# A fused attention and mixture-of-experts kernel: maxima columns by their own DMAs, row-tiled projections, earlier switch to attention

## The chip, the cores and the metric

The kernel runs on one core of one Trainium2 chip. The metric is the device time of one execution in microseconds (us). A core has a matrix engine (PE, with its weight loads PEld), a vector engine (DVE), a scalar engine (ACT), GpSimd (POOL), and SyncE (SP), which here does nothing but issue DMAs; a queue name with a q (SPq, POOLq) is the issuing side of that engine. Sixteen DMA engines carry all transfers.

## What is computed

```python
def reference(x, ...):                  # x: 8 x 1024 x 256
    xn = layernorm(x)
    s  = attn(xn)                       # layernorm with scale and bias, low-rank q and kv (128),
                                        # 16 heads of 64, rotary turn of q and k,
                                        # softmax(q k^T / 8) v, times w_out, plus the residual
    g  = silu(ffn(xn))                  # 8 experts, top 2 of them, capacity 1.25, 256 -> 1024 -> 256
    return x + s * g
```

All inputs and the output are float32.

## The kernel before, in words

The program has four stages on one core. A projection stage (`project_parts`, `pj`) normalises the tokens and writes the low-rank products, the values and the router's logits. Attention (`attend_parts`, `at`) follows from about 235 to 2650 us. The experts (`expert_parts`) and the combination follow. The routing arithmetic (`route_parts`, `rt`) is spread through the start of attention: it is a generator, and each `next(choice)` in the tensor and vector streams runs one piece.

Attention works on 64 pairs of heads (`NPAIR`, 8 batches by 8 pairs). The two heads of a pair lie on the upper and lower 64 partitions, so their matrix products run beside each other as row tiles of the array. A pair has 1024 queries in two halves (`bank`, n = 0 and 1) and 8 key tiles (`KT`), which gives 16 units u. For each unit PE computes the scores of both heads into `st[u % 2]` (`scores`, L1329), each score as three products of high and low parts (`hi`, `lo`). ACT takes the exponential into `ex` (`exps`, L1171), DVE adds the exponentials up over the keys (`add_keys`, L1035), and PE multiplies them by the values into `pv[n]` (`values`, L1366). POOL's accumulating DMAs join the two partial sums, PE turns them into denominators (L1425), SP spreads these over the partitions and back (`spread`, `broadcast`, L855 and L862), and DVE divides (`normalise`).

The loop over pairs is software-pipelined. `body(i, prev, ahead)` has eight steps, g = 0 to 7, called slots in the change's name. Each holds units 2g and 2g+1, the values of two earlier units, and two half-steps (`step_x`, `step_y`, L1387 and L1401) of another chain: for each of 8 tiles of 128 queries it finds a bound on the scores of each query, to be subtracted before the exponential. That chain goes differ (PE, `fr`), relu (`gain`, ACT L1197), add (PE), and a row maximum (`maximum`, DVE L1028, line L1033), which writes one column of `mx`, 128 partitions by 1. In body i the slots 6 and 7 of pair i run at g = 0 and 1, and slots 0 to 5 of pair i+1 at g = 2 to 7 (`slot_of`). Each slot has a column for each head: 16 columns a pair. In what follows, the two maxima of a slot are the one for head 0, at the slot's own g, and the one for head 1, one g later.

From columns to rows: when four slots (eight columns, one bank) are there, `turn_maxima` multiplies `mx[n]` by an identity on PE, into the free corner of a `pv` bank; `negate` on ACT copies it with its sign changed into `mneg`; and `max_rows` on SP (L848) sends it by two DMAs of four rows of 512 bytes into one partition for each head of `top`. The first score unit of a bank waits for that (`s_mrow`, in `scores_free`), and the first two units of each half have a fourth product, `one_row` times `top`, that adds the bound.

Projections: `body(i)` makes the keys of pair i+2 and the queries of pair i+3 out of the low-rank products. Each has two halves. The first half is a full 128-row product of three passes (`project`, PE at g = 1 for keys, at g = 5 for queries). The second half is done as row tiles beside scores (`split`, `upper_rows`, `lower_rows`, at g = 3 and g = 7): the upper and the lower 64 rows of the projection go out one after the other, each beside a score product on the other half of the array. `proj_copy` on ACT takes a half out of its `pv` bank, which must be free.

SP issues its DMAs in program order: in `body`, the loads of queries for pair i+3 (weights `w`, low-rank products `c`), the values `v` of pair i+1, the four rows of bank 1, the loads of keys for i+3, `spread` of the pair before, the rows of bank 0 of pair i+1, and at the end the store and the `broadcast` of the pair before. Within `broadcast` SP waits until the reciprocals have landed in memory, then reads them back.

Of the kernel before, what the change touches and what calls it, by code (L numbers as in the profile page):

```python
# [595 lines left out]
def route_parts(nc, ctx, keep, pj):  # L596

    with ExitStack() as tiles:
# [106 lines left out]

        def ranked(e):
            e.wait_ge(s_done, 1)
# [7 lines left out]
        return {"vector": vector, "scalar": scalar, "tensor": tensor, "ranked": ranked, "spread": spread, "done": done}  # L715


def attend_parts(nc, ctx, below, bridge, io, scr, keep, pj, rt):


    with ExitStack() as tiles:
# [27 lines left out]
        mneg = [sb(f"mneg{n}", [2 * QB, P], F32R) for n in range(NH2)]  # L749
# [3 lines left out]
        ones, osb, den, denc, recc, rec, oT, ident_r = (bridge[n] for n in ("ones", "osb", "den", "denc", "recc", "rec", "oT", "ident_r"))  # L753
# [19 lines left out]
        s_tf, s_neg = sem("tf"), sem("neg")  # L773
# [9 lines left out]
        route_at = [st[0][:, n, :] for n in range(2)]  # L783
# [48 lines left out]
        def sync(e, pj_value, pj_compressed, ex_sync):  # L832
# [15 lines left out]
            def max_rows(j, n):  # L848
                e.wait_ge(s_neg, j.n(2, n + 1))
                for h in range(2):  # L850
                    r = rows[h].start
                    e.dma_start(top[j.u][r:r + 1, bank[n]].bitcast(F32).rearrange("o (t q) -> o t q", q=P),
                                mneg[n][h * QB:(h + 1) * QB, :].bitcast(F32)).then_inc(s_mrow[n], 16)
# [21 lines left out]
            def prologue():  # L875
                for s in s_store:
                    e.sem_inc(s, 16)
                for t in range(TB):
                    pj_value(t)
                    if t == 1:  # L880
                        pj_compressed()
                pj["stored"](e)
                pj["values_stored"](e)
                load_v(At(0, 0))
                for x in (Q, K):
                    e.wait_ge(s_pr, projected(At(0, 0), x, 1))
                    load_w(At(0, 2), x)
                    e.sem_inc(s_ld[x][0], 16)
                e.wait_ge(s_init, 2)
                max_rows(At(0, 0), 0)  # L890
# [95 lines left out]
        def vector(e, ex_vector):  # L986
# [41 lines left out]
            def maximum(j, k, h, ready):  # L1028

                if k % QB == 0 and h == 0:  # L1030
                    wait(e, s_tf, j.n(2, k // QB - 1))
# [36 lines left out]
            def prologue():  # L1068
# [8 lines left out]
                for h in range(2):  # L1077
                    r = rows[h].start
                    last = e.memset(one_row[r:r + 1, :].bitcast(F32), 1.0)
                last.then_inc(s_init, 1)  # L1080
                e.tensor_copy(ident_r[:, :], keep["ident"][:, :]).then_inc(s_init, 1)
# [20 lines left out]
                for _ in range(3):  # L1102
                    next(choice)

            def body(i, prev, ahead):
# [3 lines left out]
                for g in range(NG):  # L1109
# [25 lines left out]
                    if g == 5 and most:  # L1135
                        turn_sin(two, K)
# [33 lines left out]
        def scalar(e, pj_value, ex_scalar):  # L1170
# [41 lines left out]
            def negate(j, n):  # L1212
                e.wait_ge(s_tf, j.n(2, n + 1))
                wait(e, s_mrow[n], j.n(32, 0))
                e.activation(mneg[n][:, :], pv[n][0:2 * QB, 0:P], ACT.Copy, scale=-1.0).then_inc(s_neg, 1)

            def prologue():
# [22 lines left out]
                for k in range(6):  # L1240
# [3 lines left out]
                    if k == 4:  # L1244
                        negate(first, 0)
                    if k == 5:
                        proj_copy(third, Q, 0, pv[1])
# [5 lines left out]
                proj_copy(third, Q, 1, pv[1])  # L1253
                pj["values_stored"](e)

            def body(i, prev, ahead):
                one, two, three = (i.next(d) for d in (1, 2, 3))
                more = ahead >= 1
                for g in range(NG):
                    if g == 1 and prev:  # L1260
                        out_copy(prev, 1)
# [26 lines left out]
                    if g == 1 and more:  # L1288
                        far_keys(one)
                    if g == 2 and more:  # L1290
                        high(one, K)
# [18 lines left out]
        def tensor(e, pj_value, ex_tensor):  # L1310
# [11 lines left out]
            def scores_free(i, u):  # L1322
                if u == 0:
                    e.wait_ge(s_lo, i.n(2, 2))
                if u % KT == 0:
                    e.wait_ge(s_mrow[u // KT], i.n(32, 32))
# [9 lines left out]
            def project_row(j, x, k, h, dst):  # L1336
                ws, cs = PASSES[k]
                return e.matmul(dst[:, :], w[x][j.u][rows[h], ws, :], c[x][rows[h], cs, bank[1]],
                                start=(h + k == 0), stop=(ws == 1), skip_group_check=(h == 1))

            def upper_rows(i, u, j, x, dst):

                scores_free(i, u)
                for k in range(3):
                    mm = project_row(j, x, k, 0, dst)
# [10 lines left out]
            def lower_rows(i, u, j, x, dst):  # L1356

                e.wait_ge(s_upper, i.n(2, 1 if x == K else 2))
                for k in range(3):
# [3 lines left out]
                    mm = project_row(j, x, k, 1, dst)  # L1363
# [47 lines left out]

            def turn_maxima(j, n):
# [956 lines left out]
```

## Time and profile before

| | us |
|---|---|
| median of 3 runs | 3684.16 |
| lowest and highest of the three | 3682.55, 3687.47 |
| the profiled execution | 3679.85 |
| span of its trace | 3678.3 |

| engine | busy, us | share of the span |
|---|---|---|
| PE | 3609.8 | 98% |
| PEld | 2361.3 | 64% |
| DVE | 3195.8 | 87% |
| ACT | 2763.5 | 75% |
| POOL | 1201.5 | 33% |

Busy times of an engine are of instructions that execute; waits for semaphores aren't in them. On DVE and ACT an instruction's shown duration overlaps its successor's by some tens of ns, so the sum of durations is more than the busy time. PE durations (0.39 us for a product of 512 columns) overlap far more; what a product costs is the distance from one start to the next. All times in windows and timelines count from the start of the span.

### The profile page before, as it was taken

The page shows a single profiled execution, that of the slowest core. Times are in us where ns is not written, and L with a number is a line of the kernel's source. Part 1 is how long each engine was busy: PE and PEld are TensorE (multiplying, and loading weights), DVE is VectorE, ACT ScalarE, POOL GpSimd, SP SyncE. Part 2 cuts the span into 40 slices and gives each one's busy share as a digit, 9 for nine tenths or more (in the row PEclk, how much of TensorE's full clock was granted, in tenths as well). Part 3 has the DMA queues.
Part 4 walks back from the last instruction along what each step waited for, and adds up shares of the span by engine and source line. Part 5 has one row for each costly group of instructions (what it writes and reads, how often), then busy time and mean ns, then how long its engine had stood idle before and what let it go on. Part 6 is the DMA issues. An engine that isn't in the chain of part 4 may idle for free. (4 is left out here: it accounts for less than half of the span.)

```text
span 3678.3 us, 77202 instructions
## 1 busy us (share of the span) xinstructions
PE 3609.8 (98%) x24217; PEld 2361.3 (64%) x24217; DVE 3195.8 (87%) x4341; ACT 2763.5 (75%) x4016; POOL 1201.5 (33%) x1178
## 2 busy tenths in 40 slices
PE   7989999999999999999999999999999999999999
PEld 5754444444444444444444444444699999999999
DVE  8869999999999999999999999999777777777799
ACT  5767888888888888888888888888666666666665
POOL 2202222222222222222222222222366666666500
PEclk9999999999999999999999999999999999999999
DMA  7975666666666666676766666665566666665798
GB/s 266 356 261 136 176 168 172 171 170 169 167 172 164 179 161 182 156 184 156 186 158 182 162 174 164 174 170 142 177 219 216 225 213 213 225 215 214 240 370 275
DMA packets 378436, 724.74 MB, mean 197 GB/s; under 512 B 105277, under 2 KB 253886, under 8 KB 342272
## 3 DMA queue, kind: packets, MB, share of 16 engines
q0 software_dynamic: 83504, 340.66, 36.0%
q1 hardware_dynamic: 294864, 383.23, 31.5%
q8 instruction: 35, 0.57, 0.1%
q14 instruction: 33, 0.27, 0.0%
HBM read 453.60 MB, written 138.81 MB: 161 GB/s over the span
## 5 line engine op out<-in xcount | busy, mean ns | idle before, releaser
L1176 ACT ACTIVATE at_ex<-at_st 128x1024 f32<-128x1024 f32 x1024 | 1047.7, 1024 | 195.7 <-PE at_st L1319 185.6
L1375 PE MATMUL at_pv<-at_ex,at_v 128*64 128x512 f32 x4096 | 991.6, 605 | 0.0
L1033 DVE TENSOR_REDUCE at_mx<-at_fr 128x1 fp32r<-128x512 f32 x1024 | 705.2, 689 | 227.6 <-PE at_fr L1385 179.2
L1200 ACT ACTIVATE at_fr<-at_fr 128x512 f32<-128x512 f32 x1024 | 601.2, 587 | 208.6 <-PE at_fr L1385 191.1
L1375 PEld LDWEIGHTS at_pv<-at_ex,at_v 128*64 128x64 f32 x4096 | 248.3, 136 | 470.5 <-issue 461.5
L1046 DVE TENSOR_TENSOR at_sum<-at_sum,at_ex 128x1024 f32<-128x1024 f32 x448 | 544.9, 1216 | 3.7 <-ACT at_ex L1176 3.4
L1319 PE MATMUL at_st<-at_qh,at_kh 64*128 64x512 f32 x2048 | 460.1, 399 | 9.9 <-DMA at_top<-at_mneg 2.7
L1385 PE MATMUL at_fr<-at_kfar,at_qh 64*128 64x512 f32 x1024 | 454.6, 444 | 5.9 <-DVE at_mx L1033 5.3
L1382 PE MATMUL at_fr<-at_kdif,at_qh 64*128 64x512 f32 x1024 | 456.3, 446 | 3.5 <-DVEq L674 2.5
L1382 PEld LDWEIGHTS at_fr<-at_kdif,at_qh 64*128 64x128 f32 x1024 | 188.3, 184 | 416.3 <-issue 359.5
L1319 PE MATMUL at_st<-at_ql,at_kh 64*128 64x512 f32 x2048 | 452.6, 391 | 0.0
L1319 PE MATMUL at_st<-at_qh,at_kl 64*128 64x512 f32 x2048 | 451.7, 390 | 0.0
L1913 PE MATMUL ex_o<-ex_w,ex_hT 128*128 128x256 f32 x3408 | 426.0, 285 | 0.9 <-DVE ex_out L1778 0.9
L1897 PE MATMUL ex_h<-ex_xT,ex_w 128*128 128x256 f32 x3408 | 421.1, 283 | 1.6 <-DVE ex_w L1731 1.6
L1897 PEld LDWEIGHTS ex_h<-ex_xT,ex_w 128*128 128x128 f32 x3408 | 414.1, 192 | 2.8 <-DVE ex_w L1731 1.4
L1913 PEld LDWEIGHTS ex_o<-ex_w,ex_hT 128*128 128x128 f32 x3408 | 413.2, 192 | 1.1 <-DVE ex_out L1778 1.1
L934 POOL DMA_DIRECT2D at_rotq<-at_swpq x126 | 111.4, 1030 | 858.2 <-DVE at_swpq L1001 857.6
L1831 ACT ACTIVATE ex_w<-seam_stage 128x1024 fp32r<-128x1024 f32 x142 | 142.9, 1053 | 285.9 <-PE ex_o L1913 281.7
L1703 POOL DMA_INDIRECT scr_eo<-ex_out,mid_slots x142 | 255.1, 1796 | 213.8 <-DVE ex_out L1778 178.8
L1046 DVE TENSOR_TENSOR at_sum<-at_ex 128x1024 f32<-128x1024 f32 x224 | 272.4, 1216 | 4.4 <-ACT at_ex L1176 4.4
L1319 PEld LDWEIGHTS at_st<-at_qh,at_kh 64*128 64x128 f32 x2048 | 216.7, 185 | 66.6 <-issue 35.0
L928 POOL DMA_DIRECT2D at_sum<-at_sum x95 | 88.6, 933 | 496.8 <-DVE at_sum L1046 473.5
(213 smaller groups left out, 6345.0 us busy)
## 6 DMA issues: line engine op xcount, KB each, us to landing
at_cq<-scr_c SPq DMA_DIRECT2D x62, 1024.0 KB, 6.2
at_ck<-scr_c SPq DMA_DIRECT2D x62, 1024.0 KB, 5.0
at_sum<-at_sum POOLq DMA_DIRECT2D x95, 512.0 KB, 6.1
scr_v<-pj_v SPq DMA_DIRECT2D x64, 512.0 KB, 6.9
at_v<-scr_v SPq DMA_DIRECT2D x64, 512.0 KB, 6.7
mid_rec<-scr_rec SPq DMA_DIRECT2D x256, 128.0 KB
scr_o<-mid_oT SPq DMA_DIRECT2D x64, 512.0 KB
at_rotq<-at_swpq POOLq DMA_DIRECT2D x126, 256.0 KB, 4.6
```

What stands on the lines that cost most here:

```text
L1033: e.reduce_max(mx[k // QB][:, h * QB + k % QB:h * QB + k % QB + 1], fr[h][:, :], AX.X).then_inc(s_tr[h], 1)
L1046: e.tensor_tensor(out=acc, in0=ex[k - 1][:, :, :] if first else acc, in1=ex[k][:, :, :], op=ALU.add).then_inc(s_sum, 1)
L1176: e.activation(ex[k][:, :, :], st[u % 2][:, :, :], ACT.Exp, scale=SCALE).then_inc(s_exp, 1)
L1200: e.activation(fr[h][:, :], fr[h][:, :], ACT.Relu).then_inc(s_pos[h], 1)
L1319: return e.matmul(st[u % 2][:, h, :], kk[rows[h], keys], qq[rows[h], bank[n]], start=(t == 0 and kt < 2), stop=(t == score_terms(u)[-1]), ...
L1375: mm = e.matmul(pv[n][rows[h], :], v[i.u][:, kt, rows[h]], ex[kt][:, h, :], start=(kt == 0), stop=(kt == KT - 1))
L1382: return e.matmul(fr[h][:, :], query_tile(j, k, h), kdif[j.u][rows[h], :], start=True, stop=True)
L1385: return e.matmul(fr[h][:, :], query_tile(j, k, h), kfar[j.u][rows[h], :], start=False, stop=True, skip_group_check=True)
L1703: e.indirect_dma_start(out=scr["eo"], out_offset=bass.IndirectOffsetOnAxis(ap=slots[:, g * GT + c:g * GT + c + 1], axis=0), in_=out[g % 2] ...
L1831: e.activation(w2_half(a.u, 0, k), half2(raw2[a.u], k), ACT.Copy).then_inc(s_w2h, 1)
L1897: mm = e.matmul(phid[:, j, f % 2 * GP:(f % 2 + 1) * GP], w1[q][:, ws, f, k, :], xT[q][:, xs, k, :], start=(ws + xs + k == 0), stop=(ws == ...
L1913: mm = e.matmul(po[:, c, 0:D], hT[q][:, hh, f, c * P:(c + 1) * P], w2[q][:, ws, f, :], start=(hh + ws + f == 0), stop=(hh == 1 and f == NF ...
```

## The change

Four things, in the tensor, vector, scalar and SP streams.

1. `turn_maxima`, `negate`, `max_rows`, the tile `mneg` and the identity for it are gone. Instead SP sends each column of `mx` by a DMA of its own as soon as its maximum is made: `max_row`, 128 partitions by one float into 512 contiguous bytes of a row of `top`, 16 for each pair instead of 4. The sign moves into `one_row`, which now holds -1. The scores' wait counts 8 DMAs for each bank, and a maximum that overwrites `mx` waits for its bank's columns.
2. All four half projections of a body are row tiles, at g = 2 and 3 (keys) and g = 6 and 7 (queries). The full products at g = 1 and g = 5 are gone from the body.
3. ACT and DVE work is moved between the steps: the copy of the previous pair's output and the high part of the keys go behind the first relu of their step, the latter to g = 3; the far keys are made one body earlier, at g = 7; `low` of the queries goes from g = 1 to g = 2; at g = 5 the second turn of the keys goes ahead of an addition.
4. Before the first body, SP loads the weights of the third pair's projections after the second value tile, no longer after all stores; PE waits for one piece of the routing (`counted`), not for the rank, and the rank's wait moves to the first values of the first body; one of the routing's PSUM tiles moves from `st` to `pv`.

```diff
@@ sync @@
+            def max_row(j, k, h):
+
+                wait_apart(e, s_tr[h], j.n(NSLOT_Q, k + 1), s_apart_s)
+                r, col = rows[h].start, h * QB + k % QB
+                e.dma_start(top[j.u][r:r + 1, k * P:(k + 1) * P].bitcast(F32), mx[k // QB][:, col:col + 1].bitcast(F32),
+                            allow_slow_non_contiguous=True).then_inc(s_mrow[k // QB], 16)
...
                     if t == 1:
                         pj_compressed()
+                        e.wait_ge(s_made, 4)
+                        for x in (Q, K):
+                            e.wait_ge(s_pr, projected(At(0, 0), x, 1))
+                            load_w(At(0, 2), x)
+                            e.sem_inc(s_ld[x][0], 16)
+                for k in range(6):
+                    for h in range(2 if k < 5 else 1):
+                        max_row(At(0, 0), k, h)
                 pj["stored"](e)
                 pj["values_stored"](e)
                 load_v(At(0, 0))
...
+                one = i.next(1)
                 if ahead >= 3:
                     load(i.next(3), Q)
+                max_row(i, 5, 1)
+                max_row(i, 6, 0)
                 if ahead:
-                    load_v(i.next(1))
-                max_rows(i, 1)
+                    load_v(one)
+                max_row(i, 6, 1)
+                max_row(i, 7, 0)
+                max_row(i, 7, 1)
+                if ahead:
+                    max_row(one, 0, 0)
+                    max_row(one, 0, 1)
                 if ahead >= 3:
                     load(i.next(3), K)
+                if ahead:
+                    max_row(one, 1, 0)
+                    max_row(one, 1, 1)
+                    max_row(one, 2, 0)
                 if prev:
                     spread(prev, (0, 1))
                 if ahead:
-                    max_rows(i.next(1), 0)
+                    max_row(one, 2, 1)
+                    for k in (3, 4):
+                        for h in range(2):
+                            max_row(one, k, h)
+                    max_row(one, 5, 0)
@@ vector body @@
                     if g < 2 or more:
                         maximum(*slot_of(i, g), 0, s_y)
+                    if g == 5 and most:
+                        turn_sin(two, K)
                     for added in late:
                         add_keys(*added)
-                    if g == 1 and more:
+                    if g == 2 and more:
                         low(one, Q)
...
-                    if g == 5 and most:
-                        turn_sin(two, K)
@@ scalar body @@
                     if g < 2 or more:
                         gain(*slot_of(i, g), 0, s_x)
+                    if g == 1 and prev:
+                        out_copy(prev, 1)
+                    if g == 3 and more:
+                        high(one, K)
                     exps(i, 2 * g)
                     if g < 2 or more:
                         gain(*slot_of(i, g), 1, s_y)
+                    if g == 2 and ahead >= 2:
+                        proj_copy(two, K, 0, pv[1])
+                    if g == 6 and ahead >= 3:
+                        proj_copy(three, Q, 0, pv[0])
+                    if g == 7 and ahead >= 2:
+                        far_keys(two)
                     exps(i, 2 * g + 1)
...
-                    if g in (1, 3) and ahead >= 2:
-                        proj_copy(two, K, g // 2, pv[1])
-                    if g == 2:
-                        negate(i, 1)
-                    if g in (5, 7) and ahead >= 3:
-                        proj_copy(three, Q, (g - 5) // 2, pv[0])
-                    if g == 6 and more:
-                        negate(one, 0)
+                    if g == 3 and ahead >= 2:
+                        proj_copy(two, K, 1, pv[1])
+                    if g == 7 and ahead >= 3:
+                        proj_copy(three, Q, 1, pv[0])
@@ tensor @@
                 def split(g):
 
-                    if g == 3 and ahead >= 2:
-                        e.wait_ge(s_neg, i.n(2, 2))
-                        return two, K, pv[1]
-                    if g == 7 and ahead >= 3:
-                        e.wait_ge(s_neg, one.n(2, 1))
-                        return three, Q, pv[0]
...
+                    if g == 2 and ahead >= 2:
                         if prev:
                             e.wait_ge(s_osb, i.n(2, 0))
                         else:
                             e.wait_ge(s_raw[Q], 6)
+                        return two, K, 0, pv[1]
+                    if g == 3 and ahead >= 2:
+                        e.wait_ge(s_raw[K], two.n(2, 1))
+                        return two, K, 1, pv[1]
+                    if g == 6 and ahead >= 3:
+                        e.wait_ge(s_osb, i.n(2, 1))
+                        return three, Q, 0, pv[0]
+                    if g == 7 and ahead >= 3:
+                        e.wait_ge(s_raw[Q], three.n(2, 1))
+                        return three, Q, 1, pv[0]
...
-                    if g == 1 and ahead >= 2:
-                        project(two, K, 0, pv[1])
-                    if g == 2:
...
-                        turn_maxima(i, 1)
...
                 e.wait_ge(s_init, 2)
-                rt["ranked"](e)
+                rt["counted"](e)
```

## Rows read from the trace of the kernel before

**Rows 1.** Windows: stretch, us, busy PE, PEld, DVE, ACT, POOL, PE clock, DMA share, GB/s

```profile
1200.00:1500.00 300.00, 299.01 (x1844) 148.46 (x1842) 273.39 (x325) 245.14 (x357) 74.53 (x88) 1.00 0.66 170
```

**Rows 2.** Timeline of PE (start, us, what): the first product of each step g, one `step_y`

```profile
1207.69 0.49 PE L1382 MATMUL at_fr<-at_kdif,at_qh 64*128 64x512 f32 x1
...
1212.50 0.49 PE L1382 MATMUL at_fr<-at_kdif,at_qh 64*128 64x512 f32 x1
...
1216.58 0.49 PE L1382 MATMUL at_fr<-at_kdif,at_qh 64*128 64x512 f32 x1
...
1218.30 0.39 PE L1385 MATMUL at_fr<-at_kfar,at_qh 64*128 64x512 f32 x1
...
1221.17 0.50 PE L1382 MATMUL at_fr<-at_kdif,at_qh 64*128 64x512 f32 x1
...
1225.57 0.49 PE L1382 MATMUL at_fr<-at_kdif,at_qh 64*128 64x512 f32 x1
...
1230.78 0.50 PE L1382 MATMUL at_fr<-at_kdif,at_qh 64*128 64x512 f32 x1
...
1234.84 0.50 PE L1382 MATMUL at_fr<-at_kdif,at_qh 64*128 64x512 f32 x1
...
1239.43 0.50 PE L1382 MATMUL at_fr<-at_kdif,at_qh 64*128 64x512 f32 x1
```

**Rows 3.** Timeline of PE: what else stands in the steps g = 5, 6 and 1

```profile
1209.74 0.97 PE L1421 MATMUL at_pv<-at_cq,at_wq 128*128 128x512 f32 x3
...
1214.55 0.23 PE L1415 MATMUL at_pv<-mid_ident_r,at_mx 128*8 128x128 f32 x1
1214.71 1.94 PE L1375 MATMUL at_pv<-at_ex,at_v 128*64 128x512 f32 x8
...
1226.37 0.40 PE L1319 MATMUL at_st<-at_qh,at_kl 64*128 64x512 f32 x2
1226.89 0.50 PE L1319 MATMUL at_st<-at_qh,at_kh 64*128 64x512 f32 x2
```

**Rows 4.** Timeline of DVE at g = 5 and the start of g = 6

```profile
1208.23 0.69 DVE L1033 TENSOR_REDUCE at_mx<-at_fr 128x1 fp32r<-128x512 f32 x1 [0.87 <-PE at_fr L1385]
...
1211.70 1.22 DVE L1001 TENSOR_TENSOR at_swpk<-at_rawk,at_sin 128x1024 f32<-128x1024 f32 x1
1213.04 0.69 DVE L1033 TENSOR_REDUCE at_mx<-at_fr 128x1 fp32r<-128x512 f32 x1
```

**Rows 5.** Timeline of SP's queue, same pair: issues of DMAs

```profile
1206.96 3.82 SPq L860 DMA_DIRECT2D mid_denc<-mid_den  x4
...
1225.93 3.27 SPq L869 DMA_DIRECT2D mid_rec<-scr_rec  x4
...
1231.74 0.61 SPq L846 DMA_DIRECT2D at_v<-scr_v  x1
...
1234.71 1.34 SPq L852 DMA_DIRECT2D at_top<-at_mneg  x2
```

**Rows 6.** By tile: issues (min/median/max ns) of two small DMAs

```profile
L852 SPq DMA_DIRECT2D at_top<-at_mneg x256: 572/636/773, 238.1 to 2603.7; - x128
...
L860 SPq DMA_DIRECT2D mid_denc<-mid_den x256: 544/597/2057, 315.6 to 2643.0; - x128
```

**Rows 7.** Windows of 1 us: columns as in Rows 1

```profile
1237.00:1238.00 1.00, 1.00 (x8) 0.38 (x6) 1.00 (x3) 1.00 (x2) 0.00 (x0) 1.00 0.13 40
1283.00:1284.00 1.00, 1.00 (x11) 0.56 (x7) 1.00 (x2) 0.97 (x2) 0.88 (x1) 1.00 0.13 4
```

**Rows 8.** Tile `top`: engines that waited for it over the whole run (us, times)

```profile
  PE at_st L1319: 2.7, 2
```

**Rows 9.** Timelines of PE and of SP's queue where attention begins

```profile
241.23 1.62 PE L1421 MATMUL at_pv<-at_cq,at_wq 128*128 128x512 f32 x3 [6.96 <-DMA at_wq<-scr_w]
...
249.42 0.76 PE L1382 MATMUL at_fr<-at_kdif,at_qh 64*128 64x512 f32 x1 [2.52 <-DVEq L674]
...
236.72 0.70 SPq L834 DMA_DIRECT2D at_wq<-scr_w  x1
```

More of the change, by code:

```diff
@@ L713, in done @@
             e.wait_ge(s_done, 3)
-        return {"vector": vector, "scalar": scalar, "tensor": tensor, "ranked": ranked, "spread": spread, "done": done}
+        return {"vector": vector, "scalar": scalar, "tensor": tensor, "counted": counted, "ranked": ranked, "spread": spread, "done": done}
 def attend_parts(nc, ctx, below, bridge, io, scr, keep, pj, rt):
@@ L782, in attend_parts @@
         Q, K = 0, 1
-        route_at = [st[0][:, n, :] for n in range(2)]
+        route_at = [st[0][:, 0, :], pv[0][:, :]]
         def projected(j, x, n):
@@ L1030, in maximum @@
                 if k % QB == 0 and h == 0:
[L1031 removed]
+                    wait(e, s_mrow[k // QB], j.n(32 * QB))
                 e.wait_ge(ready, j.n(NSLOT_Q, k + 2 - (h == 0)))
@@ L1101, in prologue @@
                         next(choice)
-                for _ in range(3):
+                for _ in range(2):
                     next(choice)
@@ L1244, in prologue @@
                     if k == 4:
-                        negate(first, 0)
+                        proj_copy(third, Q, 0, pv[1])
                     if k == 5:
-                        proj_copy(third, Q, 0, pv[1])
+                        proj_copy(third, Q, 1, pv[1])
                     gain(first, k, 1, s_y)
@@ L1277, in body @@
                         den_copy(prev, 1)
-                    if g in (1, 3) and ahead >= 2:
-                        proj_copy(two, K, g // 2, pv[1])
-                    if g == 2:
-                        negate(i, 1)
-                    if g in (5, 7) and ahead >= 3:
-                        proj_copy(three, Q, (g - 5) // 2, pv[0])
-                    if g == 6 and more:
-                        negate(one, 0)
+                    if g == 3 and ahead >= 2:
+                        proj_copy(two, K, 1, pv[1])
+                    if g == 7 and ahead >= 3:
+                        proj_copy(three, Q, 1, pv[0])
                     if g == 0 and more:
                         high(one, Q)
-                    if g == 1 and more:
+                    if g == 1 and more and not prev:
                         far_keys(one)
-                    if g == 2 and more:
-                        high(one, K)
                     if g == 3 and not more:
@@ L1410, in step_y @@
                 differ(j, k, 1).then_inc(s_y, 1)
-            def turn_maxima(j, n):
-                for h in range(2):
-                    e.wait_ge(s_tr[h], j.n(NSLOT_Q, QB * (n + 1)))
-                e.matmul(pv[n][0:2 * QB, 0:P], mx[n][:, :], ident_r[:, :], start=True, stop=True).then_inc(s_tf, 1)
             def project(j, x, n, dst):
@@ L1472, in prologue @@
                         pj_value(2 * k + 2)
-                    if k in (3, 4):
+                    if k == 3:
+                        e.wait_ge(s_raw[K], 4)
+                        project(third, Q, 0, pv[1])
+                    if k == 4:
                         next(choice)
-                    if k == 4:
+                    if k == 5:
                         e.wait_ge(s_raw[K], 3)
-                        e.wait_ge(s_init, 3)
-                        turn_maxima(first, 0)
+                        next(choice)
                     step_y(first, k)
@@ L1497, in bank_free @@
                         e.wait_ge(s_raw[Q], two.n(2, 2))
+                    elif n == 0 and prev:
+                        e.wait_ge(s_osb, i.n(2, -1))
                     elif n == 0:
-                        e.wait_ge(s_neg, i.n(2, 1))
+                        rt["ranked"](e)
                     elif prev:
@@ L1550, in side @@
                         half_denominators(i, 0)
-                    if g == 6 and ahead:
-                        if ahead >= 3:
-                            e.wait_ge(s_raw[Q], three.n(2, 1))
-                        else:
-                            e.wait_ge(s_osb, i.n(2, 1))
-                        turn_maxima(one, 0)
                 def lagging(u):
```

73 lines of the change are left out of this document (21 added, 52 removed).

## The prediction

> **What bounds the kernel now.** I read the windows first. In 300 us from the middle of attention PE is busy for 299.0, DVE for 273.4 (91%) and ACT for 245.1 (82%), at the full PE clock [rows 1]. PE is the bound, DVE is close behind, and a shorter PE stream can gain little more than a tenth before DVE sets the pace. A busy share doesn't say that PE's time is needed, so the timeline of PE came next, with the first product of each step of `body` [rows 2]. From 1207.69 on the steps are g = 5, 6, 7, 0, 1, 2, 3, and they last 4.81, 4.08, 4.59, 4.40, 5.21, 4.06 and 4.59 us. The reader is to see that they differ, and by what stands in them: g = 5 a full projection, g = 6 and 2 a turn of maxima, g = 7 and 3 a row-tiled projection, g = 1 a full projection and a hole. Third, SP's queue and the sizes of its issues [rows 5, 6], since the change moves the maxima there. Last, the start of attention [rows 9].
>
> **Removed from PE: the turns.** The turn begins at 1214.55 and the values behind it at 1214.71 [rows 3], so it costs 0.16 us. A plain step is then 4.08 - 0.16 = 3.92 (g = 6) or 4.06 - 0.16 = 3.90 (g = 2). 128 turns by 0.16 are 20.5 us, all on PE's path. ACT also loses two small copies a pair; ACT isn't the bound, so that counts nothing.
>
> **Full projections become row tiles.** The full one costs 4.81 - 3.92 = 0.89 (its three products show as 0.97 together, overlapping the next work [rows 3]). The row-tiled one costs 4.59 - 3.92 = 0.67 at g = 7 and 4.59 - 3.90 = 0.69 at g = 3; I take 0.68. The gain is 0.21 for each of 62 key and 61 query halves: 25.8 us.
>
> **The hole at g = 1.** Unit 3's scores start 0.52 us after the product before them (1226.37 to 1226.89 [rows 3]); they stand behind the wait for the output copy that frees `pv[1]`. What g = 1 has beyond a plain step and a full projection is 5.21 - 3.90 - 0.89 = 0.42. The change asks for the same bank one step later, 3.9 us on, when the copy, even one relu (some 0.6 us) later, is long done. 61 bodies by 0.42 are 25.6 us. Sum on PE: 71.9 us, or 1.16 a pair.
>
> **What is late next: DVE at g = 5 and 6.** In g = 5 DVE has a maximum, a turn by the cosine, a maximum, an addition and a turn by the sine. The first starts 0.54 us after the step (1208.23 against 1207.69), and the last ends its slot at 1212.83 (1211.70 plus 1.22 less 0.09 of overlap), 5.14 after the step's start. Today that is in time: the next maximum starts at 1213.04, when PE has made its input [rows 2, 4]. With g = 5 cut to 3.92 that input is there at 3.92 + 0.54 = 4.46, and DVE is 0.68 late. It ends that maximum near 5.75. PE needs it in `step_y` of g = 6, which now is a row-tiled step, and there `step_y` stands 1.72 after the step's start (1216.58 to 1218.30 [rows 2]), so at 3.92 + 1.72 = 5.64. With the hand-over PE waits some 0.25 us. Bounds: 0, if the hand-over is hidden, and 0.68, if PE takes the whole lateness. I take 0.25, nearest to the start times, and 61 by 0.25 are 15.3 us lost. By the same count g = 2 and 3 are just full: DVE has 4.6 us of work in each against 4.6 of PE. ACT's copies and high parts come in steps with at most 4.3 us of work (two relus, two exponentials and 1.45 of the rest) against 4.59; I cost these moves at nothing. Their cover is the distance of one unit between an exponential and the scores that reuse its `st`.
>
> **Added on SP: 16 columns for 4 rows.** No row shows a DMA from 128 partitions to one. The nearest is `mid_denc`, one partition to 128, with 128 short pieces too: 0.60 us in the median of issue, 2.06 at most; the four together took 3.82 here, 0.96 each, the last of them behind full DMA queues [rows 5, 6]. The removed rows took 0.64. A column is then 0.60 to 0.96, and I take 0.60 in quiet stretches. For each pair that is 9.6 to 15.4 us of SP in place of 2.6. What matters is the tightest deadline, bank 1 before the scores at g = 4. Counted from g = 0 (1221.17): the broadcast's last issue ends at 1229.20 (+8.0), and the values' load at 1232.35 (+11.2) [rows 5]. With five columns between and behind, the last is issued by +14.2 at 0.60 each, or +16.0 at 0.96. Its maximum is there by about +10, so SP, not DVE, is last. The scores at g = 4 start at +18.26 now (1239.43) and at +17.5 with the shorter steps (4.40 + 3.90 + 4.58 + 4.59). Before, the last row was issued by 1236.05 (+14.9), and PE waited for rows only twice in the run [rows 8], so issue to landing took under 3.4 us. By 1237 (+15.8) the big loads ahead were through, at a DMA share of 0.13 [rows 7]. At 0.60 a column there are 3.3 us for landing: enough. At 0.96 there are 1.5, and some half a microsecond is missing. I take 0, with 0.5 as the other end. Bank 0 has its last maximum some 8 us before its deadline, ahead of `broadcast` in the queue. Behind SP's new waits stand the key loads, `spread` and `broadcast`; each wait ends before the event that these wait for themselves, and the loads are used a body later.
>
> The DMA engines: the window at 1283 holds only spread pieces of 16 bytes, 4 KB or 256 of them at a share of 0.13 of 16 engines [rows 7], so 0.13 x 16 / 256 = 8.1 ns each. 2048 pieces a pair are 1.04 us of all engines, 3% beside a share of 0.66 [rows 1]. That hides, unless a 4-byte write costs several times a 16-byte one, and no row excludes it.
>
> The Trainium skill, DMA: Bandwidth & Descriptors, Rules for kernel authors, speaks against this part: join many small transfers into one large, and avoid a strided last dimension, which becomes one descriptor for each element. By it the change pays; that is the third rival, and the trace so far bears it out only under full queues.
>
> **The switch.** PE stands 6.96 us for weights that SP issues at 236.72, behind the last stores, and 2.52 more for the rank [rows 9]. After the idle time three products take 1.62 us against 0.97 [rows 3, 9], at the lower of PE's two clock levels. The loads now go out earlier and the rank isn't awaited, so the first body could start near 239, not at 249.4; the limit is then eight columns on SP behind the value stores. But routing pieces move into the first body, where DVE has the most to do. I take 8 us; bounds 3 (most of it given back there) and 13 (the slow clock goes too).
>
> **The sum.** 71.9 - 15.3 + 8 = 64.6 us off the profiled execution's 3679.85 gives 3615.3. The median of the runs lies 4.3 above that execution, so I forecast a median of 3620.
>
> **The rivals.**
> 1. DVE's lateness isn't absorbed: PE pays 0.68 each pair, 41.5 us, and the saving is 71.9 - 41.5 + 8 = 38.4: 3646. For: DVE at 91%, full steps at g = 2 and 3. Against: g = 6 leaves DVE over a microsecond to catch up, and PE needs a maximum only later in the step.
> 2. Columns slightly late: at 0.96 each PE waits 0.5 at g = 4 of each pair, 30.5 us on top of the forecast: 3650. For: the stretch from +8 to +16 has full DMA queues. Against: the median issue of 0.60.
> 3. Columns dear, slower than before: a column costs 1.3 us on SP in that stretch. The last is issued at +11.2 + 6.5 = +17.7, lands 2 us later (an estimate under the 3.4 above) at +19.7, and PE waits 2.2 each pair, 134 us: 3684 - 80 + 134 = 3738. It decides from 1.12 us a column, where the wait, 1.3 us, eats 71.9 + 8. For: the 2.06 of one issue. Against: three of four issues at 0.6.
> 4. Everything hidden, the switch at 13: 84.9 off, 3599.
> 5. The change doesn't take effect, because the hole and DVE's waits move to other steps and use up the gain: 3684. The only thing for it is how close DVE is; its idle 9% speaks against.
>
> **Chances.** Forecast 0.55, rivals 1 to 5: 0.17, 0.10, 0.09, 0.06, 0.03. The forecast's own range is 3605 to 3635 (0 to 0.5 of DVE, 3 to 13 of the switch); with rivals 1, 2 and 4 it is 3598 to 3655. The measurement of this kernel tells 0.2%, 7 us, from no change: faster 0.87, within it 0.04, slower 0.09.
>
> **What would show it.** In the changed trace g = 1 and 5 should last 3.9 us, g = 2, 3, 6 and 7 about 4.6 (g = 6 up to 4.9, with a wait for a maximum), a body 36.2, and the first body should start near 240. A column's issue should be 0.6 us with few waits of PE on `top`. Wrong would be: waits for `top` at g = 4 in each body, issues over 1 us, DVE above 95% with PE waiting at the starts of steps, or ACT ending its exponentials later than the scores that need `st`.

## The result, and the profile after

The changed kernel takes 3785.9 us in the median of four runs (3770.7 to 3803.9) against 3683.4 for the kernel before (3681.4 to 3687.5). The ratio is 1.028, with a 95% interval of 1.023 to 1.033: slower by 102 us, where 64 us less were forecast. Its profiled execution took 3788.99 us with a span of 3787.4. A single run of it scatters by 0.9%, of the kernel before by 0.2%.

The engine rows of the page and the windows of the middle of attention, the latter with the columns of [rows 1]:

```profile
PE 3614.7 (95%) x24458; PEld 2385.7 (63%) x24458; DVE 3181.3 (84%) x4340; ACT 2744.4 (72%) x3888; POOL 1196.4 (32%) x1178
...
1200.00:1500.00 300.00, 283.79 (x1762) 143.16 (x1763) 253.62 (x304) 227.30 (x319) 71.89 (x86) 0.98 0.66 154
```

PE has lost 15 of 299 us to waiting, and its mean clock is 0.98. DVE and ACT are less busy than before, so neither took over as the bound. What PE waits for is in its group of scores (busy, mean ns, then idle before it and the releaser), and in the waits of the whole run (us, times, longest):

```profile
L1333 PE MATMUL at_st<-at_qh,at_kh 64*128 64x512 f32 x2048 | 513.9, 403 | 111.4 <-DMA at_top<-at_mx 111.4
...
PE at_st L1333 <- DMA at_top<-at_mx: 111.4, 61, 9.2
PE at_fr L1401 <- DVE at_mx L1052: 16.3, 68, 2.4
```

The columns are late, once in nearly every body: 111.4 us, where [rows 8] had 2.7. The second line is DVE's lateness, some 0.17 us a body. The timeline of PE around g = 3, 4, 5 and 6 of one body shows where:

```profile
1232.83 0.50 PE L1398 MATMUL at_fr<-at_kdif,at_qh 64*128 64x512 f32 x1
...
1234.77 0.50 PE L1333 MATMUL at_st<-at_qh,at_kh 64*128 64x512 f32 x2 [1.43 <-DMA at_top<-at_mx]
...
1239.89 0.49 PE L1398 MATMUL at_fr<-at_kdif,at_qh 64*128 64x512 f32 x1
...
1243.80 0.50 PE L1398 MATMUL at_fr<-at_kdif,at_qh 64*128 64x512 f32 x1
...
1245.86 0.47 PE L1401 MATMUL at_fr<-at_kfar,at_qh 64*128 64x512 f32 x1 [0.18 <-DVE at_mx L1052]
...
1248.86 0.50 PE L1398 MATMUL at_fr<-at_kdif,at_qh 64*128 64x512 f32 x1
```

The step from 1232.83 to 1239.89 is g = 4, 7.06 us long. PE finished what it had and then stood idle for 1.43 us in front of its scores. The next, g = 5, lasts 3.91, and g = 6 lasts 5.06.

The same reading for some 40 bodies (timelines from 600 to 2100 us, mean distance from one step's first product to the next) gives this table. The last column is of an experiment below.

| step | before | forecast | changed | columns first, addition moved |
|---|---|---|---|---|
| g = 0 | 4.40 | 4.40 | 4.38 | 4.36 |
| g = 1 | 5.21 | 3.90 | 3.91 | 3.93 |
| g = 2 | 4.06 | 4.58 | 4.61 | 4.60 |
| g = 3 | 4.59 | 4.59 | 4.62 | 4.63 |
| g = 4 | 5.40 | 5.40 | 8.19 | 5.37 |
| g = 5 | 4.81 | 3.92 | 3.91 | 3.91 |
| g = 6 | 4.07 | 4.85 | 5.06 | 4.63 |
| g = 7 | 4.60 | 4.60 | 4.60 | 4.60 |
| body | 37.14 | 36.24 | 39.30 | 36.03 |

All steps but g = 4 and 6 came out within 0.04 us of the forecast. The loss is in g = 4: 2.79 us. 1.78 of these are the recorded wait (67.8 us in 38 bodies). Most of the rest is PE's clock. Windows of 2 us around another wait, which ended at 1195.05, show the granted clock (third number from the end) after it:

```profile
1192.00:1194.00 2.00, 1.12 (x6) 0.19 (x2) 2.00 (x4) 1.51 (x3) 0.19 (x1) 1.00 0.91 132
1194.00:1196.00 2.00, 0.95 (x8) 0.84 (x10) 0.98 (x1) 0.00 (x0) 1.59 (x2) 1.00 0.93 370
1196.00:1198.00 2.00, 2.00 (x18) 1.15 (x18) 0.00 (x0) 1.02 (x1) 0.00 (x0) 0.64 1.11 269
1198.00:1200.00 2.00, 2.00 (x12) 0.34 (x12) 1.94 (x3) 1.51 (x2) 0.00 (x0) 0.51 0.68 129
1200.00:1202.00 2.00, 2.00 (x10) 0.61 (x11) 0.48 (x1) 0.67 (x2) 0.89 (x1) 1.00 0.14 21
```

PE waited 1.93 us, and soon after the clock went from 2.4 to 1.2 GHz for over 3 us, in which each product takes twice as long. It doesn't happen each time. The same view behind a wait of 1.94 us, after the row of PE that ends it:

```profile
1474.80 0.50 PE L1333 MATMUL at_st<-at_qh,at_kh 64*128 64x512 f32 x2 [1.94 <-DMA at_top<-at_mx]
...
1474.00:1476.00 2.00, 1.20 (x10) 1.05 (x12) 0.73 (x1) 0.00 (x0) 1.32 (x2) 1.00 0.88 348
1476.00:1478.00 2.00, 2.00 (x18) 0.74 (x16) 0.82 (x2) 1.85 (x3) 0.00 (x0) 1.00 1.06 252
1478.00:1480.00 2.00, 2.00 (x14) 0.56 (x10) 1.60 (x2) 1.18 (x2) 0.42 (x1) 1.00 0.77 138
```

The step of the first of these waits lasts 9.12 us, that of the second 7.57. Of the 38 bodies 18 have the slow stretch, all with waits of 1.82 us or more. The 15 with shorter waits have none, and neither have five with waits of 1.93 to 2.54. In an experiment below it also followed a wait of 1.61, so these runs give no limit. So a wait near 2 us costs 2.2 us of step without the slow clock and 3.7 with it, and on average the slow clock is some 0.8 of the 2.79. The 0.2 left are in each step that waits, with or without the slow clock: 7.06 less 5.40 is 1.66 for a recorded wait of 1.43.

SP's queue in the body of the first timeline (start, us of issue):

```profile
1227.73 0.65 SPq L847 DMA_DIRECT2D at_v<-scr_v  x1
...
1229.88 0.53 SPq L853 DMA_DIRECT2D at_top<-at_mx  x1
```

The second row is the last column of bank 1. It was issued by 1230.41, or +15.1 after g = 0 (1215.29), and landed at 1234.77, or +19.5, when PE went on. The issue is cheap: 0.48 us in the median of 1024. 63 of them took over 1 us, up to 4.5, nearly all the first column behind `spread`, far from the deadline of its bank. The landing is late. In the 38 bodies of the table it came at +19.8 on average, 4.8 us after the issue, and the values' load, which stands ahead in the queue, landed at +19.1.

### The profile page after: what moved, and what is told of

Its sections match the earlier page's. It is cut to its first block and busy times, and to the rows that moved or that the text cites. A ratio compares the mean times of both kernels' runs of the same rounds, so it can differ in the third digit from the quotient of the medians.

```text
span 3787.4 us, 79729 instructions
## 1 busy us (share of the span) xinstructions
PE 3614.7 (95%) x24458; PEld 2385.7 (63%) x24458; DVE 3181.3 (84%) x4340; ACT 2744.4 (72%) x3888; POOL 1196.4 (32%) x1178
## 3 DMA queue, kind: packets, MB, share of 16 engines
q1 hardware_dynamic: 440272, 383.30, 33.9%
## 5 line engine op out<-in xcount | busy, mean ns | idle before, releaser
L1333 PE MATMUL at_st<-at_qh,at_kh 64*128 64x512 f32 x2048 | 513.9, 403 | 111.4 <-DMA at_top<-at_mx 111.4
L1333 PE MATMUL at_st<-at_qh,at_kl 64*128 64x512 f32 x2048 | 509.2, 399 | 0.0
L1333 PE MATMUL at_st<-at_ql,at_kh 64*128 64x512 f32 x2048 | 507.2, 397 | 0.0
L1401 PE MATMUL at_fr<-at_kfar,at_qh 64*128 64x512 f32 x1024 | 464.4, 453 | 17.2 <-DVE at_mx L1052 16.3
L1398 PE MATMUL at_fr<-at_kdif,at_qh 64*128 64x512 f32 x1024 | 465.9, 455 | 1.8 <-DVE at_mx L1052 0.9
L953 POOL DMA_DIRECT2D at_rotq<-at_swpq x126 | 111.4, 1031 | 801.7 <-DVE at_swpq L1020 801.0
L1333 PEld LDWEIGHTS at_st<-at_qh,at_kh 64*128 64x128 f32 x2048 | 241.3, 187 | 164.1 <-issue 117.5
```

Of the source, the lines that this page charges most:

```text
L1333: return e.matmul(st[u % 2][:, h, :], kk[rows[h], keys], qq[rows[h], bank[n]], start=(t == 0 and kt < 2), stop=(t == score_terms(u)[-1]), ...
L1398: return e.matmul(fr[h][:, :], query_tile(j, k, h), kdif[j.u][rows[h], :], start=True, stop=True)
L1401: return e.matmul(fr[h][:, :], query_tile(j, k, h), kfar[j.u][rows[h], :], start=False, stop=True, skip_group_check=True)
```

## The experiments

**The order alone.** All that stands ahead of bank 1's columns on SP goes behind them:

```diff
-                if ahead >= 3:
-                    load(i.next(3), Q)
                 max_row(i, 5, 1)
                 max_row(i, 6, 0)
-                if ahead:
-                    load_v(one)
                 max_row(i, 6, 1)
                 max_row(i, 7, 0)
                 max_row(i, 7, 1)
+                if ahead >= 3:
+                    load(i.next(3), Q)
+                if ahead:
+                    load_v(one)
```

> The changed kernel, with only the order of SP's DMAs in a body changed: the five columns of bank 1 go out ahead of the query loads and of the value load. In the changed kernel step g = 4 lasts 8.2 us on average against 5.4 before, with 1.8 us of PE waiting for columns. Theory 1 (a column can't land before the 1.5 MB of loads queued ahead of it on the same queue; values issued at +12.4 land 6.8 us later, at +19.2, and the scores want the columns at +17.5): the wait is gone, g = 4 lasts 5.4, a body 36.5 us and the whole about 3786 - 61 x 2.8 = 3615 us. Theory 2 (128 pieces of 4 bytes take some 4.3 us to land, whatever stands ahead): the last column, issued near +11.9, lands by +16.2, so the wait is gone here too. Theory 3 (the mass of pieces slows all transfers, wherever they stand): PE keeps waiting over 1 us for columns or for the moved loads, 3700 or more.

Measured: 3633.6 us (3633.0 to 3634.7), ratio to before 0.987 (0.985 to 0.989). g = 4 lasts 5.36 and a body 36.47. Its waits for the columns in the whole run:

```profile
PE at_st L1333 <- DMA at_top<-at_mx: 7.5, 2, 5.8
```

So the wait is a matter of place in the queue, and its end makes the change a gain of 1.3%. The two waits left are those of the first and the last body. Theory 3 falls as it was put, since PE no longer waits. The 19 us above the expectation come from its count: it took 61 times the 2.8 us of the middle bodies, 171 us, but over all 62 bodies between the first and the last the step g = 4 fell by 152 us in sum (484.5 to 332.6), and 3786 less 152 is 3634.

**Only the values behind.**

```diff
                 if ahead >= 3:
                     load(i.next(3), Q)
                 max_row(i, 5, 1)
                 max_row(i, 6, 0)
-                if ahead:
-                    load_v(one)
                 max_row(i, 6, 1)
                 max_row(i, 7, 0)
                 max_row(i, 7, 1)
+                if ahead:
+                    load_v(one)
```

> As the one before, but only the value load (0.5 MB) goes behind the five columns; the query loads (1 MB) stay ahead. Theory 1: the load ahead lands some 6.6 us after its issue at +10, so at +16.6, ahead of the deadline at +17.5: PE waits under 0.3 us in a body, 3615 to 3640. Theory 2: the last column is issued near +14.5 and lands at +18.8, PE waits 1.3 us and more for the clock, near 3700.

Measured: 3659.8 us in one run. g = 4 lasts 5.80 on average, and 16 of some 40 bodies wait, by 0.77 us. Between the two expectations, nearer to the first: both loads count, and the larger share is that of the values, the last one ahead.

**One piece for a column.** The row `one_row` is read in place of the column (the maxima are left out, and the exponential's scale is a thousandth):

```diff
-                e.dma_start(top[...], mx[k // QB][:, col:col + 1].bitcast(F32), ...)
+                e.dma_start(top[...], one_row[r:r + 1, :].bitcast(F32))
```

> The changed kernel with its order of DMAs, but each column DMA reads a constant row of 128 contiguous floats in place of a column (so the real maxima are left out, and the exponential's scale is cut to keep its values finite). The count of DMAs, their bytes and their places in the queue stay, and the 128 pieces of the source are gone. Theory 1: PE waits for these rows as for the columns, 1.8 us in a body, about 3786 us. Theory 2 and theory 3: the waits are gone, about 3615.

Measured: 3653.9 us in one run, g = 4 at 5.60 with 6 waits in 40 bodies. The packets of SP's queue fall from 440272 to 325584, by 112 for each DMA, so it went as 16 pieces, not 128. Theory 1 as it stood, the loads ahead and nothing else, falls: with the same loads ahead most of the waits went. Two causes act together. The values' load ahead also lands sooner here, 5.2 us after its issue in the median against 6.8 in the changed kernel, so the pieces delay that load as well as themselves. By which way they do isn't shown.

**Columns in the kernel before.** Part 1 of the change alone: `max_row` in the change's order, -1 in `one_row`, no turns and no copies of them (waits that counted these copies now count what frees the same bank); the projections stay where they were.

> The kernel before with one part of the change alone: columns sent by their own DMAs in the change's order, no turns, no negated copies; the full projections stay at g = 1 and g = 5. The scores at g = 4 then want their columns at +18.2, not at +17.5. Theory 1: the values ahead of the columns land at +19.2, PE waits about 1 us in a body and pays for the clock after it, less 0.16 us saved twice: 3700 to 3730 us. If the columns cost nothing by themselves and only the shorter steps brought the deadline forward: 3684 - 20 = 3664.

Measured: 3734.0 us (3726.9 to 3743.5), ratio 1.015 (1.013 to 1.017), just above the 3700 to 3730 of theory 1. g = 4 lasts 6.37 against 5.40, with 31 waits in 40 bodies. The steps without their turn last 3.92 (g = 2) and 3.90 (g = 6), which confirms the 0.16 us of a turn. The columns are late without the shortened g = 1. The earlier deadline of the full change then adds to it.

**Landings, measured by SP itself.** A wait behind the last issue of bank 1 makes SP's own waiting the time to landing:

```diff
                 max_row(i, 7, 1)
+                wait_apart(e, s_mrow[1], i.n(32 * QB, 32 * QB), s_apart_s)
```

In the changed kernel, in the one with one piece for a column, in the one with the loads behind, and, after `max_rows(i, 1)` and with a count of 32, in the kernel before:

> The changed kernel with a wait on SP behind the last column of bank 1, so that SP's next issue shows when that column landed. With the loads reordered the waits of PE had gone, and with the 128 pieces of each column replaced by one row most of them had gone too, in the old order. Theory 1 (the loads queued ahead set the landing): from the last issue's end to SP's next issue some 4.4 us, the same as PE saw in the changed kernel (1230.4 to 1234.7). The added wait only moves the key loads, which aren't urgent, so the time stays within 3750 to 3800 us. Rival (what delays the columns is what stands behind them, the key loads that share the DMA engines): with these held back the columns land in 2.5 us and PE's waits shrink, under 3700 us.

> The same wait on SP in the kernel that sends a constant row of 128 contiguous floats in place of each column (real maxima left out, the exponential's scale cut). If the loads ahead set the landing alone, the rows land as late as the columns, 4.4 us after the last issue. If the pieces count, the rows land earlier by their share: PE's waits had fallen from 1.8 us in a body to some 0.2, so 2.5 to 3 us.

> The same wait on SP in the kernel that sends the five columns of bank 1 ahead of the query and value loads. No large load of SP's queue stands ahead now. If the pieces are slow by themselves: over 4 us from the last issue to SP's next. If it is the place in the queue: 2 to 2.5 us. The loads start later by as much; PE should still not wait, 3630 to 3640 us.

> The kernel before with a wait on SP behind the four rows of bank 1, which shows when they land. The prediction allowed under 3.4 us from issue to landing and took the loads ahead to be through at +15.8. In the other runs a column behind the loads landed 3.9 us after its issue (with the key loads held back) and 1.6 us with no load of SP's queue ahead. Theory (rows behind loads are as late as one-piece columns there): 2.5 to 3.3 us from the last row's issue at +14.9, so they land at +17.4 to +18.2, and the kernel before had under 1 us to spare before its scores at +18.3. Rival (they landed early, near +17): 2 us or less. The time stays at 3683 in both.

Measured, SP's waits of the whole run in this order (us, times, longest), 3718.3, 3664.9, 3634.8 and 3684.2 us for the kernels in one run each:

```profile
SPq L80 <- DMA at_top<-at_mx: 247.3, 64, 11.6
```

```profile
SPq L80 <- DMA at_top<-at_one_row: 211.9, 64, 5.5
```

```profile
SPq L80 <- DMA at_top<-at_mx: 102.8, 64, 8.5
```

```profile
SPq L80 <- DMA at_top<-at_mneg: 153.3, 64, 5.4
```

Divided by 64: a column lands 3.86 us after its issue behind the loads, a row of 16 pieces there 3.31, a column ahead of the loads 1.61, and the kernel before's rows 2.40. So with the key loads held back the place in the queue is worth 2.25 us and the pieces 0.55 (2.2 and 0.5 without the last body, which has the longest wait of each). The kernel before had its rows by +14.9 + 2.4 = +17.3, 1.0 us ahead of the first product of g = 4 at +18.26. The scores that need them start 0.34 us later:

```profile
1239.77 0.40 PE L1319 MATMUL at_st<-at_qh,at_kh 64*128 64x512 f32 x2
```

The margin of the kernel before was thus 1.3 us. The kinds foretold came out, the sizes did not quite: 3.31 lies between the 4.4 of the loads alone and the 2.5 to 3 of the pieces, 1.61 is under the 2 to 2.5 of the place in the queue, and 2.40 is just under the 2.5 to 3.3 of rows that are late too. In the changed kernel both sides held in part: the column landed after 3.86, not 4.4, and the kernel was 68 us faster, which it should not have been. The wait there also holds the key loads back, so these were the next suspect.

**The key loads later.**

```diff
-                if ahead >= 3:
-                    load(i.next(3), K)
                 if ahead:
                     max_row(one, 1, 0)
                     max_row(one, 1, 1)
                     max_row(one, 2, 0)
+                if ahead >= 3:
+                    load(i.next(3), K)
```

> The changed kernel, with only the key loads of a body (1.1 MB, issued right behind the columns of bank 1) moved behind three later columns, so by some 3 us. The loads ahead of bank 1's columns stay. Theory (loads ahead set the landing alone): PE waits as in the changed kernel, g = 4 at 8.2 us, 3770 to 3800 us. Rival (with the columns held up behind the loads, the key loads that start right behind them share the engines and add 1 us; the kernel with SP's wait, which also held them back, had landings of 3.9 us against 4.9): g = 4 near 6.6, 3700 to 3730 us.

Measured: 3749.8 us (3746.1 and 3753.5), ratio 1.018 (1.015 to 1.021), g = 4 at 7.21 against 8.19. PE's wait fell from 1.78 to 1.31 us a body, so 0.5 us of the 1.0 is an earlier landing; the other half is the slow clock, which 6 of 39 bodies have in place of 18 of 38. The rival was right in kind and expected more (g = 4 near 6.6): what SP issues behind the columns delays them too. How a later transfer of the same queue holds up an earlier one isn't settled by these runs.

**DVE's addition.** In step g = 5 DVE's one addition goes to the start of g = 6, first in the changed kernel, then in the one with the loads behind:

```diff
                     early, late = additions(i, prev, g)
+                    if g == 5:
+                        late = ()
+                    if g == 6:
+                        early = ((i, 1, 1), *early)
```

> The changed kernel with only the one addition moved from g = 5 to g = 6 on DVE. Theory (the steps g = 5 to 7 lie outside the stretch from the reciprocal to the scores of g = 4 in which the columns are late, so a shorter g = 6 isn't given back): g = 6 at 4.63, g = 4 still at 8.2, 61 x 0.43 = 26 us less, 3745 to 3775. Rival (the wait at g = 4 takes it back): g = 4 grows by 0.4, 3786.

> The reordered kernel (columns of bank 1 ahead of the query and value loads), and on DVE the one addition of step g = 5 moved to the start of g = 6. Step g = 6 lasts 5.06 us there against 4.60 of the other row-tiled steps, with PE waiting 0.17 us in each body for a maximum and the rest unexplained by a wait. Theory (DVE comes late out of g = 5, where it has 4.6 us of work against 3.9 of PE): with the addition gone from g = 5, g = 6 lasts 4.6, a body 36.0 us, and the whole 3634 - 61 x 0.46 = 3606 us. Rival (g = 6 is long for another reason, such as the output copy ahead of the relu on ACT): g = 6 stays at 5.06 and the time at 3634. Rival on the other side (the moved addition makes the maxima of g = 6 or 7 late): over 3640.

Measured: alone 3739.0 us (3724.9 and 3753.1), ratio 1.015 (1.006 to 1.024), with g = 6 at 4.61; with the loads behind 3610.9 us (3608.6 to 3612.5), ratio to before 0.980 (0.979 to 0.982), with g = 6 at 4.63. DVE's lateness was the whole cause of the long step. Alone, g = 4 fell to 7.62 as well, which neither side expected. The wait is nearly what it was, 1.66 us a body, but the slow clock follows in 8 of 39 bodies only. How often it follows varies from run to run: the two here, 28 us apart, have mean granted clocks of 0.989 (3753.1 us) and 0.994 (3724.9), so little can be said of this sum. The second kernel is faster than both the kernel before and the changed one, by 72 and 175 us. In its middle of attention no PE wait is left:

```profile
1200.00:1500.00 300.00, 300.00 (x1930) 153.63 (x1928) 279.73 (x333) 249.76 (x350) 83.63 (x91) 1.00 0.73 179
```

DVE is at 93% and ACT at 83%, the DMA engines at 0.73.

**The switch.** In that fastest kernel, the stores, the first values and the third pair's weights go out in the order of before the change, ahead of the first columns:

```diff
                     if t == 1:
                         pj_compressed()
-                        e.wait_ge(s_made, 4)
-                        for x in (Q, K):
...
+                pj["stored"](e)
+                pj["values_stored"](e)
+                load_v(At(0, 0))
+                for x in (Q, K):
+                    e.wait_ge(s_pr, projected(At(0, 0), x, 1))
+                    load_w(At(0, 2), x)
+                    e.sem_inc(s_ld[x][0], 16)
                 for k in range(6):
                     for h in range(2 if k < 5 else 1):
                         max_row(At(0, 0), k, h)
-                pj["stored"](e)
-                pj["values_stored"](e)
-                load_v(At(0, 0))
```

> The reordered kernel with the moved addition, with one part of the switch undone: SP loads the third pair's weights after the value stores again, as before. Theory (PE's stall of 7 us at the start of attention comes from these weights, and the slow clock after it): the stall is back at the first full projection of the third pair, and the time is 8 to 11 us longer, 3619 to 3622. Rival (the first body waits for columns or for the routing on DVE anyway): 3611 to 3614.

Measured: 3624.0 us (3621.5 to 3626.7), ratio to before 0.984 (0.982 to 0.985), so 13 us more than with the early loads. In the profiled executions 10.6 of these lie at the start (the second body begins at 294.7, not at 284.1), the rest mostly in the last body's wait for columns (8.1 us for 5.6). The stall is back, and at the lower clock behind it three products take 1.62 us again, as in [rows 9]:

```profile
241.83 1.62 PE L1435 MATMUL at_pv<-at_cq,at_wq 128*128 128x512 f32 x3 [12.23 <-DMA at_wq<-scr_w]
```

In the changed kernel itself the first body began here, waited once for bank 0, and its first scores already ran at the lower clock (0.79 for 0.40):

```profile
238.43 0.47 PE L1398 MATMUL at_fr<-at_kdif,at_qh 64*128 64x512 f32 x1 [0.83 <-DVE rt_need L662]
...
241.04 0.79 PE L1333 MATMUL at_st<-at_qh,at_kh 64*128 64x512 f32 x2 [2.12 <-DMA at_top<-at_mx]
```

## Why the prediction was wrong

It failed in one step, and that step turned the sign.

**The step that failed: "I take 0" for the lateness of bank 1's columns.** The issues were priced well: one each 0.65 us in this stretch (five in 3.23), and 0.48 in the median, where 0.60 to 0.96 was taken, and the last one ended at +15.1 where +14.2 to +16.0 stood. The landing was wrong. The prediction read from a DMA share of 0.13 at 1237 [rows 7] that the loads ahead were through at +15.8. But the values were issued at 1231.74 [rows 5], and this load takes 6.8 us in the changed kernel (by its tile; 6.7 in the kernel before) from issue to landing, so it is through near 1238.4, +17.3. A quiet window doesn't show a landing. In the change two columns stand between the loads, and the values go out at +12.4, not +10.6. On average they landed at +19.1 and the last column at +19.8, where PE would have begun its scores at +17.9. Issue times and the bound "under 3.4 us" said nothing on that. The measured margin of the kernel before was 1.3 us, of which the shorter steps alone take 0.8. The term taken at 0 measured 2.79 us a body in the middle of attention: 1.78 of waiting, and the clock and the restart after it.

**What stood for the price of a miss.** Rival 2 had the right place, and 0.5 us in place of 1.8. Rival 3 had the right sign and the wrong cause: it wanted issues over 1.12 us, and the issues were cheap. Neither counted the slow clock, which followed 18 of 38 waits and made a step 1.6 us longer. The trace of before had that effect once, behind the stall of [rows 9], and the prediction used it there, not for the loop. The 109 us between the two profiled executions add up: the second body starts 8.5 us earlier (284.2 for 292.7), the 62 bodies from there on take 110 us more, and the rest takes 7 more, which is the last body's wait for columns (9.19 us for 2.47; the fastest version still has 5.6). Of the 110, g = 4 makes 149, and the other steps give back 39 where 57 were forecast; 13 of that difference are g = 6.

**The rule that spoke against it.** The Trainium skill, DMA: Bandwidth & Descriptors, Rules for kernel authors, to join small transfers and avoid a strided last dimension, was weighed at 0.09. The runs bear it out, as a second cause beside the place in the queue. With the key loads held back the pieces cost 0.55 us of landing, the place 2.25. In the change's own order they cost more: one piece in place of 128 let PE wait in 6 of 40 bodies instead of all, and took 132 us off. So either repair alone, the order or the pieces, does most of it. The engines' own time for a piece is an estimate of 12 ns, by the shares of the queue in two kernels of different order (34.8% of 3631.4 us with the loads behind, against 32.2% of 3652.3 with one piece, 16 engines, 114688 pieces); 8.1 was the prediction's.

**What was right.** The 0.16 us of a turn, 0.89 for a full projection against 0.68 for a row-tiled one, and the hole at g = 1, with all four sums: 1.16 us were forecast, and 37.14 less 36.03 are 1.11 once DVE and the columns are out of the way. DVE late at g = 5 and 6 was right in place and cause; a maximum was forecast to end 5.75 after the start of g = 5 and ended at 5.83 (1245.72 less 1239.89). Its price was 0.46, not 0.25, inside the bounds given: `step_y` starts 2.06 us after g = 6 does where 1.73 is usual, with 0.18 of that a recorded wait, and the rest comes with the restart behind it. ACT's moves cost nothing that a wait shows. The switch's start at 239 was right (238.4), and so was its worth: 8.5 us at the second body, where 8 were taken (10.6 for the early weights and their order alone, in the fastest kernel). The first body didn't use all of the earlier start, since PE waits 2.12 us for bank 0 there and then runs at the lower clock.

With bank 1's columns ahead of the loads the same change measures 3633.6, where the forecast was 3620; the difference is mostly the 0.2 us by 61 of g = 6, some 13 us. This agreement stands on the order of the DMAs, which the prediction did not foresee.

## What to carry to other kernels

A small DMA that an engine is waiting for has to be costed by its landing, and behind large loads of the same queue take it as not before theirs: the last load's issue plus its time to landing, from its own tile's row. Before shortening a loop, measure how much margin each transfer has against its deadline; a wait on the issuing engine behind it shows that in one run. It cost the kernel before nothing (3684.2 us), but it holds back what stands behind it in the queue, and in the changed kernel that alone took 68 us off. Urgent small transfers go ahead of loads that are wanted a loop later.

## What the runs showed of the hardware

- A DMA from 128 partitions, one float each, into one row issues in 0.48 us and lands 1.6 us later ahead of the loads, 3.9 us behind 1.5 MB of them, and 4.8 us with another 1.1 MB issued behind it.
- Columns of 128 short pieces also slow the large load among them: 512 KB of values landed 6.8 us after their issue in the changed kernel and 5.2 us with one row in place of each column.
- Transfers issued later on the same queue delay earlier ones: moving 1.1 MB of key loads behind three more columns took 0.5 us off PE's wait (1.78 to 1.31 us), and 0.5 off the slow clock after it.
- The clock fell from 2.4 to 1.2 GHz after a wait of 1.93 us in a stream otherwise busy, and didn't after one of 1.94 or 1.43 us. In 38 bodies of the changed kernel, with waits of 0.2 to 3.0 us, it fell after 18, and a fall made the step 1.6 us longer.
